# A four-layer graph network kernel: rows moved before the first product, and both products made from one turned operand

## The reference

```
layer 0: x + softplus-MLP(sum over a node's edges of 160 attributes)
layer 1: (x @ Wself.T + bself + mean-of-neighbours @ Wneigh.T + bneigh) / 2
layer 2: relu(x @ ws + sum of (x @ wn)[src])
layer 3: Chebyshev, K = 3, 128 -> 256 -> relu -> 128, with w = -deg^-1/2 deg^-1/2
```

## Time and profile before

| | us |
|---|---|
| median of 3 runs | 4638.28 |
| lowest and highest | 4631.76, 4641.12 |
| the profiled execution | 4677.37 |
| its span | 4675.5 |

### The profile page before, as it was taken

The page is one execution under the profiler, slowest core; times in us unless marked ns, Lnnn a source line. Parts: engine busy times, 40 slices in busy tenths (PEclk is TensorE's granted clock), DMA queues, the critical chain, the costliest instruction groups (busy, mean ns, idle before and its releaser), DMA issues.

```text
span 4675.5 us, 74892 instructions
## 1 busy us (share of the span) xinstructions
PE 3326.4 (71%) x20670; PEld 2625.1 (56%) x20670; DVE 3077.4 (66%) x12829; ACT 2499.1 (53%) x7360; POOL 3168.9 (68%) x3630
## 2 busy tenths in 40 slices
PE   2278977777999999999995655657868867821111
PEld 0135646666888888888884554654436667721111
DVE  2398978997888888888884665771223435545545
ACT  0005668997888888888884551114546633311111
POOL 6405658876888888888884554646656646566666
PEclk6598888999999999999997777888989989955555
DMA  0005544663222222222222433445657756633222
GB/s 21 4 6 171 171 134 167 216 215 107 78 76 76 78 78 74 78 78 74 78 74 81 123 121 100 135 126 177 225 183 263 267 198 211 219 103 92 87 84 75
DMA packets 311878, 575.84 MB, mean 123 GB/s; under 512 B 69502, under 2 KB 97975, under 8 KB 311466
## 3 DMA queue, kind: packets, MB, share of 16 engines
q1 hardware_dynamic: 235178, 443.56, 28.3%
q0 software_dynamic: 76288, 127.51, 10.1%
HBM read 301.23 MB, written 271.14 MB: 122 GB/s over the span
## 4 chain that ended last, share of the span: by engine, by line
DVE 41%; issue 17%; PE 16%; another core or an unknown queue 13%; POOL 6%; ACT 5%; DMA 1%; DVEq 0%; SPq 0%; ACTq 0%; POOLq 0%; PEldq 0%; PEld 0%
DVE bn L969 11%; DVE y L1023 5%; DVE mv L974 4%; PE ps L1444 3%; POOL rows L563 3%; DVE u L1037 3%; DVE y L1043 2%; POOL out_dram L678 2%; DVE x L853 2%; DVE x3b L853 2%; PE ps L1383 2%; PE ps L1426 1%; PE ps L1401 1%; PE ps L1427 1%
## 5 line engine op out<-in xcount | busy, mean ns | idle before, releaser
L563 POOL DMA_INDIRECT rows<-state,rows_of_src x588 | 555.9, 945 | 408.2 <-issue 163.8
L853 DVE TENSOR_TENSOR_SCAN x<-same,x,ps 128x512 f32<-128x512 uint8 x336 | 429.2, 1277 | 354.5 <-remote 238.9
L1401 PE MATMUL ps<-ident,rows 128*128 128x128 f32 x1372 | 289.4, 318 | 421.4 <-ACT rows L1154 248.4
L1137 ACT ACTIVATE yTa<-ps 128x512 f32<-128x512 f32 x392 | 233.0, 594 | 611.1 <-PE ps L1383 308.7
L563 POOL DMA_INDIRECT rows<-lap,rows_of_lap x392 | 380.3, 970 | 215.7 <-issue 107.9
L1401 PEld LDWEIGHTS ps<-ident,rows 128*128 128x128 f32 x1372 | 203.7, 166 | 476.0 <-issue 251.6
L647 POOL DMA_INDIRECT lk<-node_table,look_idx x392 | 390.6, 997 | 91.9 <-issue 87.7
L1142 ACT ACTIVATE sd<-mv,consts 128x4 f32<-128x4 f32 x588 | 174.6, 297 | 493.6 <-remote 176.3
L1540 PE MATMUL ps<-V,hT 128*128 128x128 f32 x3136 | 405.4, 283 | 8.7 <-ACT hT L1273 8.7
L969 DVE BATCH_NORM_STATS2 bn<-y 128x6 f32<-128x128 f32 x1764 | 380.4, 280 | 23.5 <-POOL y L599 23.4
L1540 PEld LDWEIGHTS ps<-V,hT 128*128 128x128 f32 x3136 | 368.0, 193 | 46.0 <-ACT hT L1273 42.8
(11 more groups left out here) (269 smaller groups left out, 9346.7 us busy)
## 6 DMA issues: line engine op xcount, KB each, us to landing
state_h<-hb SPq DMA_DIRECT2D x98, 512.0 KB
xin<-in_x_dram SPq DMA_DIRECT2D x196, 256.0 KB
out_dram<-outb SPq DMA_DIRECT2D x196, 256.0 KB
xe<-state SPq DMA_DIRECT2D x147, 256.0 KB
state<-outb SPq DMA_DIRECT2D x98, 256.0 KB
state<-oe SPq DMA_DIRECT2D x98, 256.0 KB
h_pre<-hb SPq DMA_DIRECT2D x49, 512.0 KB
rows<-in_edge_attr_10x_dram SPq DMA_DIRECT2D x48, 320.0 KB
```

Of the source, the lines that this page charges most:

```text
L563: gp.indirect_dma_start(out=dest[:, at, k, 0:width], out_offset=None, in_=table_, in_offset=bass.IndirectOffsetOnAxis(ap=index[:, c:c + 1] ...
L853: v.tensor_tensor_scan(t[0:np_, g.b].rearrange("p k d -> p (k d)"), same[0:np_, 512 * g.c:512 * g.c + 512], ps[0:np_, bk + g.b, :], t[0:np ...
L1401: i = t.transpose(bank(g.b)[:, k, :], rows[:, g.r, k, 0:P], ident[:, :])
```

## The change

The division by a row's deviation after the first product is left out in the node stage. What comes instead: VectorE adds to each row of y0 the value (deviation - mean), so that the row's mean is its deviation; the product with the new matrix `A1b` (A1 plus b1c/128 in each row) then gives the product plus deviation times b1c, that is the old y1 times the deviation. The new matrix `AWb` is A1b @ ws, so that both products come from the same turned rows. `y1`, its transposes and `yTb` go. The sum of squares is made by ScalarE straight from PSUM, once u2 is made, and in the node stage VectorE multiplies the small constant of the root by the variance (`tq2`). u2 is now made by two VectorE instructions, a max and an add.

In `src0` the rows are normalised as before into `outb` and those are turned. In the node stage y0 has four buffers, GpSimd makes it two blocks ahead, not one, and TensorE turns block g-1 in turn g. SyncE's functions are not touched. The setup has one more transpose, two more products and three more copies.

```diff
+        A1b, AWb = sb("A1b", [P, P]), sb("AWb", [P, P])
+        y0_ring = (y0[:, 0], y0[:, 1], y1[:, 0], y1[:, 1])
+        PRODUCTS = ((3, 4), (7, 1))
...
             def make_y0(p, g):
-                (x_in if p == "nodes" else x_gathered).wait(pool, p, g)
-                y0_turned.wait(pool, p, g, back=2)
+                if p == "nodes":
+                    x_in.wait(pool, p, g)
+                    y0_turned.wait(pool, p, g, back=RING)
+                    gp.tensor_tensor(y0_ring[g.r], xin[:, g.b], all4(c0h[:, :]), ALU.add).then_inc(y0_made.sem, 1)
+                    return
+                x_gathered.wait(pool, p, g)
                 bn0.wait(pool, p, g, back=2)
                 gp.tensor_tensor(y0[:, g.b], xin[:, g.b], all4(c0h[:, :]), ALU.add).then_inc(y0_made.sem, 1)
...
-                    next_, g2, g3 = g.less(-1), g.less(2), g.less(3)
+                    next_, g2, g3 = g.less(-2 if p == "nodes" else -1), g.less(2), g.less(3)
...
             enter(pool, "nodes")
             make_y0("nodes", Turn(0))
+            make_y0("nodes", Turn(1))
...
+            def moved(g, out_ap):
+
+                return v.tensor_tensor(out_ap, sd[:, 0, g.b, :], mv[:, 0, g.b, :, 0], ALU.subtract)
...
+            def src0_turn(g):
+                p, n = "src0", QUADS
+                g1, g2, g3 = (g.less(k) for k in (1, 2, 3))
+                i0, i1, i2, i3 = (t.inside(n) for t in (g, g1, g2, g3))
+                if i0:
+                    y0_made.wait(dve, p, g)
+                    stats(0, y0[:, g.b], bn0)
+                    bn0.wait(dve, p, g)
+                    x1_made.wait(dve, p, g, back=2)
+                    aggregate(0, g.b, mv0)
...
+                if i0:
+                    sd0.wait(dve, p, g)
+                    v.reciprocal(rs[:, 0, g.b, :], sd[:, 0, g.b, :]).then_inc(rs0.sem, 1)
+                    moved(g, lift[:, g.b, :]).then_inc(off0.sem, 1)
...
+                if i0:
+                    rs0.wait(dve, p, g)
+                    off0.wait(dve, p, g)
+                    v.tensor_tensor(lift[:, g.b, :], lift[:, g.b, :], rs[:, 0, g.b, :], ALU.mult).then_inc(off1.sem, 1)
+                    off1.wait(dve, p, g)
+                    out_st.wait(dve, p, g, back=2)
+                    y0_turned.wait(dve, p, g, back=2)
+                    for k in range(3):
+                        i = v.tensor_scalar(outb[:, g.b, k, :], y0[:, g.b, k, :], dev(0, g.b, k), lift[:, g.b, k:k + 1],
+                                            ALU.mult, ALU.add)
+                    i.then_inc(x1_most.sem, 1)
+                if i1:
+                    own, near = PRODUCTS[g1.b]
+                    p1_made.wait(dve, p, g1)
+                    x3_made.wait(dve, p, g1, back=2)
+                    v.tensor_scalar(u2[:, g1.b], bank(near), 0.0, None, ALU.max).then_inc(u2_half.sem, 1)
+                    u2_half.wait(dve, p, g1)
+                    v.tensor_tensor(u2[:, g1.b], bank(own), u2[:, g1.b], ALU.add).then_inc(u2_made.sem, 1)
+                    u2_made.wait(dve, p, g1)
+                    stats(1, u2[:, g1.b], bn2)
+                    bn2.wait(dve, p, g1)
+                    aggregate(1, g1.b, mv2)
...
+            def nodes_turn(g):
+                y0_now = y0_ring[g.r]
+                if i0:
+                    y0_made.wait(dve, p, g)
+                    stats(0, y0_now, bn0)
+                    bn0.wait(dve, p, g)
+                    aggregate(0, g.b, mv0)
...
+                if i0:
+                    sd0.wait(dve, p, g)
+                    moved(g, rs[:, 0, g.b, :]).then_inc(off0.sem, 1)
...
+                if i0:
+                    off0.wait(dve, p, g)
+                    v.tensor_tensor(y0_now, y0_now, rs[:, 0, g.b, :].unsqueeze(2).to_broadcast([P, 4, P]), ALU.add)\
+                        .then_inc(y0_moved.sem, 1)
...
+                    p1_made.wait(dve, p, g1)
+                    x3_made.wait(dve, p, g1, back=2)
+                    v.tensor_scalar(u2[:, g1.b], bank(4), 0.0, None, ALU.max).then_inc(u2_half.sem, 1)
+                    u2_half.wait(dve, p, g1)
+                    v.tensor_tensor(u2[:, g1.b], bank(3), u2[:, g1.b], ALU.add).then_inc(u2_made.sem, 1)
+                    u2_made.wait(dve, p, g1)
+                    stats(1, u2[:, g1.b], bn2)
+                if i4:
+                    p3_made.wait(dve, p, g4)
+                    x3b_made.wait(dve, p, g4)
+                    out_made.wait(dve, p, g4, back=2)
+                    v.tensor_tensor(y3[:, g4.b], bank(7), x3b[:, g4.b], ALU.add).then_inc(y3_made.sem, 1)
+                if i1:
+                    squared.wait(dve, p, g1)
+                    v.scalar_tensor_tensor(ssum[:, g1.b, :], mv[:, 0, g1.b, :, 1], EPS * P, ssum[:, g1.b, :],
+                                           ALU.mult, ALU.add).then_inc(tq2.sem, 1)
+                    bn2.wait(dve, p, g1)
+                    aggregate(1, g1.b, mv2)
+                if i4:
+                    y3_made.wait(dve, p, g4)
+                    stats(2, y3[:, g4.b], bn3)
+                if i1:
...
+            def square(p, g, made, source):
+
+                made.wait(act, p, g)
+                tv2.wait(act, p, g, back=2)
+                squared.wait(act, p, g, back=1)
+                for k in range(4):
+                    i = a.activation(unused[:, k, :], source[:, k, :], ACT.Square, accum_out=ssum[:, g.b, k:k + 1])
+                i.then_inc(squared.sem, 1)
...
+            def nodes_turn(g):
+                p, n = "nodes", BLOCKS
+                g1, g2, g3, g4, g5 = (g.less(k) for k in (1, 2, 3, 4, 5))
+                if g1.inside(n):
+                    keep(p, g1, y0T_kept, y0_turned, [(p1_made, 1)], yTa[:, :, :], 0)
...
+                if g.inside(n):
+                    root(p, g, sd0, mv0, sd[:, 0, g.b, :], mv[:, 0, g.b, :, 1], EPS4)
+                if g4.inside(n):
+                    h_made.wait(act, p, g4)
+                    p3_made.wait(act, p, g4, back=1)
+                    for j in range(2):
+                        a.activation(hT[:, j], bank(5 + j), ACT.Relu, bias=gb1_col[:, j:j + 1]).then_inc(hidden.sem, 1)
+                if g3.inside(n):
+                    keep(p, g3, x3T_kept, x3_turned, [(h_made, 1)], yTc[:, :, :], 2)
+                if g1.inside(n):
+                    square(p, g1, u2_made, bank(3))
+                if g5.inside(n):
+                    off3_made.wait(act, p, g5)
+                    out_st.wait(act, p, g5, back=2)
+                    for k in range(4):
+                        i = a.activation(outb[:, g5.b, k, :], y3[:, g5.b, k, :], ACT.Identity,
+                                         bias=off3[:, g5.b, k:k + 1], scale=rs[:, 3, g5.b, k:k + 1])
+                    i.then_inc(out_made.sem, 1)
...
+            def products(p, g, own, near):
+
+                for k in range(4):
+                    t.matmul(bank(own)[:, k, :], yTa[:, k, :], A1b[:, :], start=True, stop=True)
+                    i = t.matmul(bank(near)[:, k, :], yTa[:, k, :], AWb[:, :], start=True, stop=True)
+                i.then_inc(p1_made.sem, 1)
...
+            def src0_turn(g):
+                p, n = "src0", QUADS
+                g1, g3 = g.less(1), g.less(3)
+                if g1.inside(n):
+                    x1_most.wait(pe, p, g1)
+                    x1_made.wait(pe, p, g1)
+                    y0T_kept.wait(pe, p, g1, back=1)
+                    turn4(p, g1, y0_turned, outb[:, g1.b], 0)
+                if g3.inside(n):
+                    x3_made.wait(pe, p, g3)
+                    x3T_kept.wait(pe, p, g3, back=1)
+                    turn4(p, g3, x3_turned, x3[:, g3.b], 2)
+                if g1.inside(n):
+                    y0T_kept.wait(pe, p, g1)
+                    u2_made.wait(pe, p, g1, back=2)
+                    squared.wait(pe, p, g1, back=2)
+                    x2_made.wait(pe, p, g1, back=2)
+                    products(p, g1, *PRODUCTS[g1.b])
+                if g3.inside(n):
+                    x3T_kept.wait(pe, p, g3)
...
+            def nodes_turn(g):
+                p, n = "nodes", BLOCKS
+                g1, g3, g4 = (g.less(k) for k in (1, 3, 4))
+                if g1.inside(n):
+                    y0_moved.wait(pe, p, g1)
+                    y0T_kept.wait(pe, p, g1, back=1)
+                    turn4(p, g1, y0_turned, y0_ring[g1.r], 0)
+                if g3.inside(n):
+                    x3_made.wait(pe, p, g3)
+                    x3T_kept.wait(pe, p, g3, back=1)
+                    turn4(p, g3, x3_turned, x3[:, g3.b], 2)
+                if g1.inside(n):
+                    y0T_kept.wait(pe, p, g1)
+                    u2_made.wait(pe, p, g1, back=1)
+                    squared.wait(pe, p, g1, back=1)
+                    products(p, g1, 3, 4)
+                if g4.inside(n):
+                    hidden.wait(pe, p, g4)
...
```

(17 more changed lines are left out.)

429 lines of the change are left out of this document (169 added, 260 removed).

## The result

The change makes the kernel slower: 5086.73 us (median of 4 runs, 5075.25 to 5101.77) against 4635.02 (4 runs on the same chip), a ratio of 1.0977 [1.094, 1.1014], +452 us. The forecast was +328 (4966 us). The direction, the place and the mechanism were right, the size of the loss was not: it is above the forecast's own range (up to 5040), and 3 us inside the wide one (up to 5090), which reached that far only because it took in rival (c). That the time lies in it at all is luck. The profiled execution took 5093.48 us, its span 5091.7.

What follows compares the result with a forecast made beforehand. The prediction took a loop through TensorE and ScalarE to bound nodes, VectorE and ScalarE being busiest in src0. Nodes +270, src0 +56 and setup +2 gave +328 on 4638, so 4966 us, range 4900 to 5040.

Steps and rivals of the forecast that it cites:

- the wide one: Whole time: the wider range, 4770 to 5090 us, taking in three of the four rivals.
- rival (c): Both stages: TensorE falls to L1's clock, +84 us in nodes and +21 in src0, 5071 us; chance 0.10.
- The two-turn loop through the late load: Nodes: xin's load behind ScalarE's output closes a loop of 16.88 us, 8.44 a turn against 7.02, +270 us.
- GpSimd's turn: Nodes: L599 to the end of L622 takes 6.69 us, a step of the loop over two turns.
- In `nodes` ... the clock costs nothing there: Nodes: TensorE's busy share stays near src0's of today, granted clock 0.98, so no time is added.
- y0_moved falls where GpSimd waits ... and costs nothing more: Nodes, VectorE: this add runs while GpSimd waits for its load, so it adds nothing beyond its 0.69 us.
- Landing 2.7: Nodes: xin's load takes 2.7 us from issue to landing, chosen between 2.3 and 3.01.
- Issue 0.41, squares and output 2.82, u2 1.59: Nodes: three steps of the loop over two turns, in us, u2 with its 0.15 hand-over from TensorE.
- src0, 8.5 us a turn, +56: In src0 ScalarE's squares wait for u2, closing a loop: 8.5 us a turn against 7.33, +56 us.
- The third loop, 7.48, hidden: Nodes: VectorE and ScalarE wait on each other twice a turn, 7.48 us, hidden under 8.44.
- Rival (d): Nodes: not slower; TensorE is the only bound, the turn falls to GpSimd's 6.69 us, -65, 4573 us; chance 0.05.

Runs made afterwards that it cites:

- runs 1 and 6: Changed kernel with SyncE loading xin three blocks ahead, not two: 1.0322; changed kernel with GpSimd's node-stage y0 asked one turn later: 1.0336.
- run 10: Changed kernel with only VectorE's copy of four elements moved behind u2 and its statistics: 4582.47 us, 1.0939, on a chip where the kernel before takes 4187.98.
- run 8: Changed kernel with 16 more identity transposes on TensorE in each node turn, ahead of its wait for x3: 5044.51 us, 1.0784.
- run 9: Changed kernel with products ahead of x3's transposes and VectorE's copy of four elements behind u2 and its statistics: 4844.18 us, 1.0371.
- runs 2 and 11: Changed kernel with squares ahead of u2's second half in both stages: 1.0687; changed kernel with earlier xin load and that order in src0 alone: 1.0216.
- Run 12: Changed kernel with earlier xin load and squares first in src0, plus the node stage's second-product Relu moved from VectorE to ScalarE: 4773.09 us, 1.0208.
- run 5: Changed kernel with the two products ahead of x3's transposes in TensorE's list of a node turn: 4976.97 us, 1.0651.

## Why the prediction was right, and where it fell short

The waits, the loop that they close and its place were forecast as the runs show them. Three terms of its sum were too small and two a little too large; they add up to 117 us, and rival (c) and the wide range covered them by chance.

- **The two-turn loop through the late load** (+270): right. Shown by undoing it from either end (runs 1 and 6, both back to 7.4 us a turn) and by its own steps in the timeline. Where clock and GpSimd's turn are as I assumed, it is 16.91 us in the mean (run 10) against 16.88. In the changed kernel two turns take 17.99 in the mean, and the stage loses +385.
- **"In `nodes` ... the clock costs nothing there"**: wrong, and the largest miss. Transposes and products take 3.24 us on the loop with their hand-over instead of 2.67, 0.57 for two turns, which is 56 of the 124 us; against the same work in run 8, at 1.00, it is 72. I had compared mean busy shares of stages, TensorE's 77% in `src0` before with its granted 0.98, and put rival (c) at 0.10. After the change the share in `nodes` is again 76% (227.65 of 300 us) and the mean clock 0.95; both hide that the work behind the pause, on the loop itself, runs at 0.50 in about half of the long turns. Rival (c) had the right sign, and 84 us for its node part. The mean clock of L1 in its sum was the wrong figure, and that it came near is luck: on the loop the clock is 0.50 in some turns and 1.00 in the others. The Trainium skill, "TensorE: Matmul & The Clock Gate", HAM oscillation — how this bites in real kernels, tells of such a pattern, a wait ahead of each block of work and each block starting at the low clock. The 0.50 behind the pause agrees in kind, but in the turn shown it came about a microsecond into the work, and the products were slow in 48 long turns of 92; I hadn't weighed it.
- **"y0_moved falls where GpSimd waits ... and costs nothing more"**: it is 0.72 us in the mean as against 0.68, so this holds for it as such. But where it meets L632 it is GpSimd that loses: the four normalisations take 2.21 us in the mean in the 87 turns in which y0_moved overlaps them, and 1.73 in the other 100. GpSimd's turn is 7.13 instead of 6.69, 43 us over the stage. And I never asked the same of the copy of four elements: 0.16 us when alone, up to 2.83 behind the end of a normalisation and two additions of GpSimd. In the changed kernel moving it gives 56 us (run 10), by way of GpSimd's turn and the clock; with the products out of the way it gives 130 (run 9).
- **Landing 2.7**: too short. It is 2.72 in the turn shown, but 3.15 in the mean of the long turns, above even the 3.01 of rows 5, and costs 44 us. Why it takes longer than where the stage begins is open.
- **Issue 0.41, squares and output 2.82, u2 1.59**: 0.41, 2.66 and 1.49 in the mean, 25 us less than forecast.
- **src0, 8.5 us a turn, +56**: measured 8.67 and +64. The cause is shown: squares first give 7.5 (runs 2 and 11). The clock is in it as well, 0.88 from 800 to 1000.
- **The third loop, 7.48, hidden**: right, it appears at 7.37 to 7.42 as soon as the load is in time. Run 12 shows that it runs through both engines.
- **Rival (d)**, TensorE alone as the bound: 100% busy it was only with 28 transposes added.
- **The sum**: 328 + 56 (clock) + 43 (GpSimd's turn) + 44 (landing) - 25 (u2, squares, output) + 8 (`src0`) = 454, against 452. These are the terms as the trace shows them. What each would give if it were taken out alone is another matter, as they move together: filling the pause shortened GpSimd's turn too, and so did moving the copy.

## What to carry to other kernels

When a step asks for its input a turn earlier, follow the request to the queue that issues the transfer, and to what the issue stands behind: if that is the output of a later step, the loop closes and its length is divided by the number of turns that it spans. Where you can, take out a wait by moving the request and not by turning it round: the reversed wait is a new edge. In `src0` it took 1.1 us off the turn; in `nodes`, with the load in time, it closed a loop of 8.26 us where there was one of 7.37. On a loop with a pause in it price TensorE's work at the clock of the microseconds behind the pause, read in windows of that size, not at the mean of the stage. And take the steps of a loop as means over many turns: the one pair that I had read had a landing of 2.72 where the mean is 3.15.

## What the runs showed of the hardware

- TensorE's granted clock fell to 0.50 about a microsecond after it had resumed from a pause of 3.8 us, and stood there for the next 3.4 us, in which it was busy. With 16 more transposes (1.9 us) in each turn it was 1.00 from 1500 to 1800.
- The pause ahead isn't all that decides. Two turns of the kernel with the change, each with the transposes of x3 and the first products behind a pause of 3.3 us:

```profile
1564.82 0.66 PE L1451 MATMUL ps<-ident,x 128*128 128x128 f32 x4 [3.28 <-POOL x L632]
...
1565.31 0.39 PE L1577 MATMUL ps<-A1b,yTa 128*128 128x128 f32 x2
...
1618.55 1.12 PE L1451 MATMUL ps<-ident,x 128*128 128x128 f32 x4 [3.36 <-POOL x L632]
...
1619.45 0.64 PE L1577 MATMUL ps<-A1b,yTa 128*128 128x128 f32 x2
```

  The first pair runs at 1.00 throughout. The second is slow from its first transpose, as there the clock had fallen while TensorE still stood idle:

```profile
1617.00:1618.00 1.00, 0.00 (x0) 0.00 (x0) 1.00 (x3) 1.00 (x2) 1.00 (x3) 0.77 0.73 246
```

  What else decides is open.
- A VectorE `tensor_scalar` of 4 elements a row, SBUF to SBUF, with one input, was held up by GpSimd's wide addition for its whole length (1.2 us), and through the end of a normalisation and two additions in a row for 2.83 us; GpSimd didn't let it in between them. The same kind of instruction with 512 elements from PSUM (L1094) took 0.68 or 0.69 us, also beside the additions (run 5, 1539.59). In my prediction only instructions with two inputs were suspected.
